# Differential attention: the two halves of the weighing on different tiles of the array, ahead of the scores, with v and y in one bank

## The reference

```python
q = apply_rope(x @ wq.T); k = apply_rope(x @ wk.T)      # 4 half heads of 64
v = (x @ wv.T)                                          # 2 heads of 128
probs = softmax(q k^T / 128 ** -0.5)                    # 4 tables of 32 x 32 per sequence
diff = probs[:, :, 0] - lam * probs[:, :, 1]            # 2 tables per sequence
attn = diff @ v
attn = attn * rsqrt(mean(attn * attn) + 1e-5) * subln_weight
return attn @ wout.T
```

## Time and profile before

| | us |
|---|---|
| median of 3 runs | 3342.03 (3341.38 to 3342.73) |
| the profiled execution, its time | 3341.55 |
| its span | 3339.5 |
| PE busy in the span | 3287.2 (98%) |
| DVE busy | 2329.3 (70%) |
| ACT busy | 1988.0 (60%) |
| POOL busy | 1796.8 (54%) |
| granted clock of TensorE, mean | 0.996 |

### The profile page before, as it was taken

The page is one execution under the profiler, slowest core; times in us unless marked ns, Lnnn a source line. Parts: engine busy times, 40 slices in busy tenths (PEclk is TensorE's granted clock), DMA queues, the critical chain, the costliest instruction groups (busy, mean ns, idle before and its releaser), DMA issues.

```text
span 3339.5 us, 103483 instructions
## 1 busy us (share of the span) xinstructions
PE 3287.2 (98%) x34647; PEld 2394.9 (72%) x34656; DVE 2329.3 (70%) x7527; ACT 1988.0 (60%) x6064; POOL 1796.8 (54%) x3701
## 2 busy tenths in 40 slices
PE   9999999999899999999999999999999999999999
PEld 7888888888666777777777777777766655555555
DVE  5677777777788667888888888878868844444443
ACT  5777777777556547777777777777765411111111
POOL 5666666666566447777777777777746500000000
PEclk9999999999999999999999999999999999999999
DMA  3111111111212231111111111111136720000000
GB/s 99 55 58 56 54 54 54 58 55 54 72 43 61 85 125 46 46 49 47 45 46 46 48 46 46 47 44 47 48 90 159 186 66 19 19 17 17 17 16 9
DMA packets 280202, 187.70 MB, mean 56 GB/s; under 512 B 117037, under 2 KB 276997, under 8 KB 280085
## 3 DMA queue, kind: packets, MB, share of 16 engines
q1 hardware_dynamic: 279797, 185.75, 19.9%
q10 hardware_dynamic: 288, 0.40, 0.1%
HBM read 145.61 MB, written 36.21 MB: 54 GB/s over the span
## 4 chain that ended last, share of the span: by engine, by line
PE 57%; DMA 3%; DVE 1%; ACT 0%; SPq 0%; issue 0%; POOL 0%; DVEq 0%; ACTq 0%; POOLq 0%
PE bank_e L2827 13%; PE c_ps_a L1100 7%; PE bank_e L2807 7%; PE b_ps_a L1066 6%; PE s_ps_a L1073 5%; PE out_ps_a L1126 3%; PE a_ps_a L1077 3%; PE c_ps_a L1077 2%; PE b_ps_a L1077 2%; PE out_ps_a L1110 2%; PE c_ps_a L1159 2%; DMA by_dim_q_r<-scratch_q 1%; PE c_ps_a L1138 1%; PE out_ps_a L1197 1%; PE c_ps_a L1149 1%; DMA scratch_q<-proj_t_q_r 1%
## 5 line engine op out<-in xcount | busy, mean ns | idle before, releaser
L1226 ACT ACTIVATE probs_a<-s_ps_a,neg_max_a 128x257 f32<-128x257 f32 x1024 | 473.7, 475 | 83.3 <-DVE neg_max_a L1346 78.5
L1280 POOL TENSOR_SCALAR probs_a<-probs_a,gated_a 128x256 f32<-128x256 f32 x1024 | 470.9, 479 | 26.4 <-POOL gated_a L1289 26.4
L1346 DVE TENSOR_REDUCE neg_max_a<-s_ps_a 128x1 f32<-128x257 f32 x1024 | 424.4, 414 | 0.0
L2870 ACT ACTIVATE gate_e<-bank_e 128x512 f32<-128x512 f32 x128 | 76.3, 597 | 486.1 <-PE bank_e L2827 459.1
L546 POOL TENSOR_SCALAR probs_i<-probs_i,inv_sum_i 128x256 f32<-128x256 f32 x512 | 242.9, 487 | 135.1 <-DVE inv_sum_i L710 130.6
L2768 POOL TENSOR_TENSOR inv_std_e<-var_eps_e,half_e 128x4 f32<-128x4 f32 x8 | 8.1, 1012 | 561.7 <-DVE var_eps_e L2884 561.7
L2994 DVE TENSOR_TENSOR hidden_e<-gate_e,bank_e 128x512 f32<-128x512 f32 x128 | 87.2, 687 | 277.5 <-PE bank_e L2827 274.8
L1345 DVE TENSOR_TENSOR self_s_a<-s_ps_a,mask_a 128x32 f32<-128x32 f32 x1024 | 186.1, 182 | 135.5 <-PE s_ps_a L1073 135.4
L530 ACT ACTIVATE probs_i<-s_ps_i,neg_max_i 128x257 f32<-128x257 f32 x512 | 235.8, 474 | 58.9 <-DVE neg_max_i L781 57.1
L373 PE MATMUL a_ps_i<-w_k_i,ctx_t_i 128*128 128x256 f32 x1024 | 252.4, 389 | 0.0
L1100 PE MATMUL c_ps_a<-w_v_a,ctx_t_a 128*32 128x256 f32 x4096 | 247.6, 382 | 0.0
(11 more groups left out here) (398 smaller groups left out, 8164.6 us busy)
## 6 DMA issues: line engine op xcount, KB each, us to landing
ctx_t_i<-in_ctx_t SPq DMA_DIRECT2D x128, 256.0 KB, 2.7
ctx_t_a<-in_ctx_t SPq DMA_DIRECT2D x128, 256.0 KB, 2.7
mask_a<-in_L_xattn_mask SPq DMA_DIRECT2D x512, 4.0 KB, 1.5
v_bd_a<-v_self_a SPq DMA_DIRECT2D x512, 8.0 KB, 1.8
x_tok_i<-in_x SPq DMA_DIRECT2D x32, 128.0 KB, 2.0
x_res_i<-in_x SPq DMA_DIRECT2D x32, 128.0 KB, 2.4
x_after<-y_tok_i SPq DMA_DIRECT2D x32, 128.0 KB, 1.8
x_tok_d<-x_after SPq DMA_DIRECT2D x32, 128.0 KB, 2.2
```

The source lines that it names most:

```text
L1226: act.activation(probs[:, t, :], s_ps[:, g, 0:K], ACT.Exp, bias=neg_max[:, t:t + 1], accum_out=row_sum[:, t:t + 1]).then_inc(exp_done, 1)
L1280: pool.tensor_scalar(probs[:, t, 0:2 * P], probs[:, t, 0:2 * P], gated[:, t:t + 1], 1.0, ALU.mult, ALU.mult).then_inc(probs_ready, 1)
L1346: dve.tensor_reduce(neg_max[:, 4 * f + g:4 * f + g + 1], s_ps[:, g, 0:K], AX.X, ALU.max, negate=True).then_inc(max_ready, 1)
```

## The change

The weighing stands ahead of the scores in TensorE's slot. Its loop runs over the sequences outside and the heads inside. Head 0 of sequence s stays on the tile (rows s, columns s); head 1 goes to the columns of sequence s + 2 (mod 4), so its output lands on that sequence's partitions, in a second bank (`av_ps` now has two). All eight matmuls count on `av_full`, before it four did. Until the output product every step works on a partition alone, so nothing of head 1 has to be moved back before ScalarE's copy attn_t: after the transposes the sequences are columns, and the copy, now two instructions of half the columns each, puts them in order (`attn_t_of`, `at_of`). The bank that this takes comes from v and y, which share one (`vy_ps`): v waits until the y of two chunks before has been read, y until v has been copied. VectorE adds y to x after ms and ahead of the softmax's sums, where it stood last in the slot.

```diff
-    qk_ps, v_ps, tx_ps, av_ps = (pb(f"{n}_ps") for n in ("qk", "v", "tx", "av"))
+    qk_ps, vy_ps, tx_ps = (pb(f"{n}_ps") for n in ("qk", "vy", "tx"))
     s_ps = pb("s_ps", (P, 2, 512))
-    qk_t_ps, y_ps = (pb(f"{n}_ps") for n in ("qk_t", "y"))
+    qk_t_ps, av_ps = pb("qk_t_ps"), pb("av_ps", (P, 2, 512))
+    v_ps, y_ps = vy_ps[:, 0:D], vy_ps[:, D:2 * D]
     at_ps, xt_ps = tx_ps[:, 0:D], tx_ps[:, D:2 * D]
+    attn_t_of, at_of = attn_t[:, :, :].rearrange("p c (h k) -> p (c h) k", h=2), at_ps.rearrange("p (g k) -> p g k", g=4)
...
                 ge(pe, v_ready, n + 1)
+                ge(pe, y_ready, n - 2)
                 for c in range(2):
-                    last = pe.matmul(v_ps[:, 0:D], xn_t[:, c, :], w_v[:, c, :], start=c == 0, stop=c == 1)
+                    last = pe.matmul(v_ps, xn_t[:, c, :], w_v[:, c, :], start=c == 0, stop=c == 1)
...
                 last.then_inc(x_full, 1)
+            if live(n - 1):
+                pe.wait_ge(diff_ready, n)
+                pe.wait_ge(v_ready, n)
+                ge(pe, attn_ready, n - 1)
+                for s in range(4):
+                    own = slice(L * s, L * s + L)
+                    for c in range(2):
+                        across = (s + 2 * c) % 4
+                        last = pe.matmul(av_ps[L * across:L * across + L, c, 0:P], diff_t[(n - 1) % 2][own, c * L:c * L + L], v[(n - 1) % 3][own, c * P:c * P + P], start=True, stop=True)
+                        last.then_inc(av_full, 1)
             if live(n):
                 pe.wait_ge(qk_t_ready, n + 1)
...
-            if live(n - 1):
-                pe.wait_ge(diff_ready, n)
-                pe.wait_ge(v_ready, n)
-                ge(pe, attn_ready, n - 1)
-                for c in range(2):
-                    for s in range(4):
-                        own = slice(L * s, L * s + L)
-                        last = pe.matmul(av_ps[own, c * P:c * P + P], diff_t[(n - 1) % 2][own, c * L:c * L + L], v[(n - 1) % 3][own, c * P:c * P + P], start=True, stop=True)
-                        if c == 1:
-                            last.then_inc(av_full, 1)
             if live(n - 2):
...
                 ge(pe, y_ready, n - 2)
+                if live(n + 1):
+                    pe.wait_ge(v_ready, n + 2)
...
-                act.activation(attn_t[:, :, :].rearrange("p c k -> p (c k)"), at_ps, ACT.Copy).then_inc(at_ready, 1)
+                act.activation(attn_t_of[:, 0::3, :], at_of[:, 0::2, :], ACT.Copy)
+                act.activation(attn_t_of[:, 1:3, :], at_of[:, 1::2, :], ACT.Copy).then_inc(at_ready, 1)
...
                 dve.tensor_scalar(ms[:, :], ss[:, :], 1.0 / P, 1e-5, ALU.mult, ALU.add).then_inc(ms_ready, 1)
+            if live(n - 2):
+                dve.wait_ge(y_full, n - 1)
+                ge(dve, stored[n % 2], 16 * ((n - 2) // 2))
+                dve.tensor_tensor(y[n % 2][:, :], y_ps, x_tok[(n - 2) % X_TILES][:, :], ALU.add).then_inc(y_ready, 1)
...
-            if live(n - 2):
-                dve.wait_ge(y_full, n - 1)
-                ge(dve, stored[n % 2], 16 * ((n - 2) // 2))
-                dve.tensor_tensor(y[n % 2][:, :], y_ps[:, 0:D], x_tok[(n - 2) % X_TILES][:, :], ALU.add).then_inc(y_ready, 1)
```

More of the change, by code:

```diff
@@ L1667, in tensor @@
                 ge(pe, y_ready, n - 2)
+                if live(n + 1):
+                    pe.wait_ge(v_ready, n + 2)
                 for c in range(2):
-                    last = pe.matmul(y_ps[:, 0:D], attn_t[:, c, :], w_o[:, c, :], start=c == 0, stop=c == 1)
+                    last = pe.matmul(y_ps, attn_t[:, c, :], w_o[:, c, :], start=c == 0, stop=c == 1)
                 last.then_inc(y_full, 1)
@@ L1676, in scalar @@
                 for h in range(2):
-                    last = act.activation(attn[:, h, :], av_ps[:, h * P:h * P + P], ACT.Copy, scale=inv_rms[:, h:h + 1])
+                    last = act.activation(attn[:, h, :], av_ps[:, h, 0:P], ACT.Copy, scale=inv_rms[:, h:h + 1])
                 last.then_inc(attn_ready, 1)
@@ L1687, in scalar @@
                 act.wait_ge(v_full, n + 2)
-                act.activation(v[(n + 1) % 3][:, :], v_ps[:, 0:D], ACT.Copy).then_inc(v_ready, 1)
+                act.activation(v[(n + 1) % 3][:, :], v_ps, ACT.Copy).then_inc(v_ready, 1)
             if n == 0:
@@ L1703, in scalar @@
             if live(n - 1):
-                act.wait_ge(av_full, 4 * n)
+                act.wait_ge(av_full, 8 * n)
                 for h in range(2):
-                    last = act.activation(squares[:, h, :], av_ps[:, h * P:h * P + P], ACT.Square, accum_out=ss[:, h:h + 1])
+                    last = act.activation(squares[:, h, :], av_ps[:, h, 0:P], ACT.Square, accum_out=ss[:, h:h + 1])
                 last.then_inc(ss_ready, 1)
@@ L1773, in vector @@
                 after_this(dve.scalar_tensor_tensor(out=diff[:, :].rearrange("p (c k) -> p c k", c=2), in0=weighed[:, 2:4, :], scalar=neg_lam[:, :], in1=weighed[:, 0:2, :], op0=ALU.mult, op1=ALU.add))
-                ge(dve, av_full, 4 * (n - 1))
+                ge(dve, av_full, 8 * (n - 1))
                 dve.transpose(diff_t[n % 2][:, :], diff[:, :]).then_inc(diff_ready, 1)
```

## The result

Seven runs each: 3353.13 us after (3348.89 to 3355.35) against 3342.03 before, a ratio of 1.0035 [1.0026, 1.0045]. The change makes the kernel slower by 11 us. The forecast was 3342.7, the range ended at 3346.6, and the slot that was to stay at 5.38 became 5.51. The profiled execution took 3351.93 us.

What follows compares the result with a forecast made beforehand. TensorE's list of 5.38 us a slot was taken as the bound, loop C replacing it at 5.38. Profiled 3341.55 + 0 + 0.4 + 0.1 gave 3342.1, 3342.4 with rounding; on the median 3342.03, +0.7 gave 3342.7, range 3340.4 to 3346.6.

Steps and rivals of the forecast that it cites:

- Weighing on other tiles: TensorE's weighing block: tiles sharing rows but not columns overlap, two rounds saved, 0.22 us a slot, block 0.58 to 0.36.
- Rival 1: No overlap across columns: weighing stays 0.58 us, loop D 5.53, loop C 5.49, total 3347.4 us; chance 10%.
- Three changes of shape ... only change places: Weighing ahead of scores on TensorE: still three array-shape changes a slot, their 0.20, 0.12 and 0.20 us only swapping places.
- list 5.16: TensorE's own work per slot after the change: 5.38 less the 0.22 us saved in weighing.
- Loop D: Scores, maximum, y's early addition, softmax, xn, x's transposes, weighing, next scores: 5.31 us a slot, hidden, at no cost.
- Loop C: Two slots from scores through ScalarE's v, attn_t, y and TensorE's list: 10.75 us, 5.38 a slot, binding.
- rival 2: Dear copies: ScalarE's attn_t pair costs 0.62 us, loop C grows 0.09 a slot, total 3345.4; chance 10%.
- Loop A: Scores, maximum, statistics, inv_std, inv_rms, ScalarE's attn, qk_raw and qk_t, next scores: 5.32 us a slot, outside TensorE's other work.
- A slot over 5.45: a wait that I have missed: Sign to look for in the measured slot length: over 5.45 us would show an overlooked wait.
- Shared bank and waits "0": v and y sharing a bank, each waiting for the other's reader: 0 us, as those releases come early enough.
- "+0.4 and +0.1": Stage's two ends: first slots 0.4 us longer by slot 3, last slot and final copies 0.1 us longer.

Runs made afterwards that it cites:

- few_xn_stats: The changed kernel without three implied TensorE waits, with xn early and statistics of chunk n+3 ahead of the scores' maximum: 0.9997 of before, slot 5.407 us.
- xn_early: The changed kernel with VectorE's normalization of chunk n+3 moved ahead of weighed, diff and diff_t: 1.0025 of before, slot 5.449 us.
- order_kept: The changed kernel with the weighing block put back behind the scores: 1.0015 of before, slot 5.325 us.
- kept_few: order_kept without the weighing's implied waits on v and attn: 0.9996 of before, slot 5.326 us.
- kept_few_stats: kept_few with the statistics of chunk n+3 moved ahead of the scores' maximum: 0.9989 of before, 3337.03 us, slot 5.225.
- bank_only: The kernel before with v and y in one bank, its two waits and y's addition early: 1.0015 of before, slot 5.377 us.
- pad28: The kernel before with one always-met TensorE wait more per slot, on y's addition three chunks earlier: 1.0019 of before, 3348.51 us, slot 5.377.

## Why the prediction was wrong

**Weighing on other tiles: right.** Last start 0.18 after the first against 0.38, as forecast (0.16), in every kernel that weighs behind the transposes of x. Rival 1 did not happen, though the time came out beyond its 3347.4, since head 1's eight records on the same rows and other columns cost no round of their own. (In that rival's sum 5.53 less 5.38 is 0.15 and not 0.16, 0.3 us.) The Trainium skill's rule ("TensorE: Matmul & The Clock Gate", Part 3, "The mechanism"), by which a weight load overlaps only across groups of rows, is not what this block shows.

**"Three changes of shape ... only change places", list 5.16: the step that failed.** The shape changes did keep their 0.20, 0.12 and 0.20. But the scores block itself was taken as fixed, 0.28, and it takes 0.51 once it follows the weighing directly. The list in that order is 5.41 (few_xn_stats), 0.25 over the forecast (0.23 the scores, 0.02 the weighing) and longer than before's 5.38. So the move took back the whole gain of the tiles, even with no loop in its way.

**Loop D "5.31, hidden, at no cost": mis-sized by 0.20.** It measured 5.51 and bound the slot. Of the 0.20, 0.13 are the slow scores (the maximum starts 0.68 after their first start, not 0.55), 0.06 is the start of the weighing (0.37 after x's transposes, where the scores came 0.31 after them) and 0.02 the weighing itself (0.38, not 0.36), less 0.01 from the maximum to xn. The mechanism was as reckoned, and so was y's addition: the maximum to the end of xn is 4.03, 0.32 over before's 3.71. xn_early confirms the loop. The prediction had the warning in hand: it named 5.53 for this loop if the block were 0.22 longer, and then tied that to the weighing alone.

**Loop C: not the bound, and somewhat too short.** The two attn_t copies took 0.48 (1007.75 to 1008.23) against 0.44, y came 0.05 after them, and rival 2 fell. But TensorE waited only 0.03 for them, not 0.22, since the slow scores covered the rest, and what y lost was hidden by the wait for xn. Where loop D is out of the way (xn_early) two slots take 10.94, not 10.75.

**Loop A, 5.32: right.** order_kept and kept_few show 5.325 and 5.326; with the statistics taken out of it the slot falls to 5.225 (kept_few_stats). In after itself it doesn't bind (qk_t ends at 1007.62, 0.12 before the scores); in xn_early it binds every second slot, with slow scores in it. "A slot over 5.45: a wait that I have missed" was the true sign.

**Shared bank and waits "0": wrong by 6 us, outside every slot.** In the slot they cost nothing (bank_only 5.377). What they cost is 27 or 28 more instructions in TensorE's program, and 6 us in stages behind it. No row of before shows such a price, and the prediction gave the term no bound.

**The sum.** 28 slots of 0.13 are 3.7, slot 1, one slot in the middle and the last ones 1.2, together 4.9; 6 from the longer program, the mean of the groups: 10.9 of the 11.1 measured. The ends' "+0.4 and +0.1" are in the 1.2.

## What to carry to other kernels

When a block of many short matmuls is moved, price the block behind its new neighbour, not at the duration that it had behind the old one. Before calling a loop hidden, add the error of each of its terms: one at 5.31 under one at 5.38 is not hidden. And when waits or instructions are added to an unrolled program, compare the untouched stages too, with a padded copy of the old kernel beside it; waits that another one implies are worth removing.

## What the runs showed of the hardware

- Records on different tiles start 5 ns apart in the mean (32 scores in 0.16 us). When the block directly follows the 16 records of a weighing, its second half takes 43 ns a matmul (two records), 0.39 us for the 32. Four transposes' records between them are enough to end that.
- Eight 32 by 32 tiles, two to a row group, weigh 16 records of 128 columns in 0.18 us from first to last start, four tiles in 0.38.
- 27 more waits on TensorE that never hold anything cost 6.4 us (pad28, by its ratio), 56 cost 7.4; kernels with as many instructions as before or fewer show nothing of it. The loss lies in one stage 1.4 ms later, most of it as "issue" ahead of weight loads, and goes with one more 16 KB packet of kind "instruction" (74, not 73). Whether the supply of TensorE's program or where its parts lie does this is open. To part the two, the same number of instructions would have to be added behind that stage, which wasn't tried.
- The granted clock between stages differs from one execution to the next of the same kernel (6.8 or 13.7 us at the lower level around 1090), and the end of the stage took 9.94 or 11.13 us with it.
